# A mixture-of-experts layer on one core: rows come back by gathers that add into x, in place of gathers and additions on VectorE

## The reference

```python
x = x + 0.5 * ffn(layernorm(x), gate_w, experts)
x = x + attn(layernorm(x), W_in, conv_w, conv_b, A_log, D, W_out)
x = x + 0.5 * ffn(layernorm(x), gate_w, experts)

def ffn(x, gate_w, experts):               # B, N, D = 8, 2048, 256; E = 8; M = N // E = 256
    gates = sinkhorn(x @ gate_w)
    vals, idx = top_k(swapaxes(gates, -1, -2), M)      # each expert takes its 256 best tokens
    routed = x[b_idx, idx]
    outputs = (routed @ experts[e]) * vals
    return zeros_like(x).at[b_idx, idx].set(outputs)   # where several took one token, the last one stays
```

## Time and profile before

| | us |
|---|---|
| median of 3 runs | 3737.79 |
| the runs | 3739.79, 3737.79, 3731.17 |
| profiled execution, its own time | 3728.65 |
| its span, first to last instruction | 3727.1 |
| last layer (`ffn`) in it | from about 3315 to the end, 412 |
| busy in the span: PE, DVE, ACT, POOL | 2784.6, 3116.6, 2123.0, 1322.5 |

### The profile page before, as it was taken

How to read it: one execution, slowest core, us unless ns; L and a number is a source line. 1 busy time by engine, 2 the same in 40 slices (tenths; PEclk the granted TensorE clock), 3 DMA queues, 4 the chain that set the end, 5 groups by cost and what they waited for, 6 DMA issues and landing times. The chain is left out here.

```text
span 3727.1 us, 29733 instructions
## 1 busy us (share of the span) xinstructions
PE 2784.6 (75%) x9244; PEld 1530.2 (41%) x9244; DVE 3116.6 (84%) x2640; ACT 2123.0 (57%) x2277; POOL 1322.5 (35%) x897
## 2 busy tenths in 40 slices
PE   8703688899889799889988978987896687025653
PEld 4502333354345346435434534633442445024442
DVE  6797579999999999999999999999999566982222
ACT  6301467876877877787687787777767263001111
POOL 0002254436345344443734534450111100025665
PEclk9655799999999999999999989999998896557776
DMA  7202277688678778868867878886776462034666
GB/s 275 105 0 85 72 179 178 145 181 183 150 163 168 174 173 167 183 145 182 185 150 162 167 170 173 169 178 121 141 144 123 86 257 108 0 109 130 224 219 243
DMA packets 146619, 574.71 MB, mean 154 GB/s; under 512 B 22144, under 2 KB 73920, under 8 KB 99776
## 3 DMA queue, kind: packets, MB, share of 16 engines
q0 software_dynamic: 77136, 399.56, 51.6%
q1 hardware_dynamic: 69360, 173.68, 12.7%
HBM read 154.72 MB, written 117.51 MB: 73 GB/s over the span
## 5 line engine op out<-in xcount | busy, mean ns | idle before, releaser
L1143 DVE TENSOR_TENSOR_SCAN state<-state,drive 128x2048 f32<-128x2048 f32 x512 | 2224.3, 4404 | 54.0 <-ACT state L1341 53.7
L1341 ACT ACTIVATE state<-delta,neg_a 128x2048 f32<-128x2048 f32 x512 | 1019.4, 2005 | 230.3 <-DMA state<-state 95.7
L1555 PE MATMUL ps_states<-state,ident 128*128 128x512 f32 x1800 | 856.4, 621 | 109.5 <-DMA state<-state 94.8
L1034 POOL DMA_DIRECT2D state<-state x256 | 234.9, 919 | 1314.1 <-DVE state L1143 1303.7
L1491 PE MATMUL ps_proj<-x1t,w_in 128*128 128x512 f32 x1024 | 505.0, 637 | 90.6 <-ACT xc L1290 32.3
L1555 PEld LDWEIGHTS ps_states<-state,ident 128*128 128x128 f32 x1800 | 348.7, 200 | 516.5 <-issue 385.5
L1507 PE MATMUL ps_proj<-conv_in,tap 128*128 128x512 f32 x1024 | 488.1, 628 | 53.9 <-ACT conv_in L1262 33.0
L982 POOL DMA_INDIRECT picked<-normed_rows,slot_now x112 | 355.9, 3178 | 99.1 <-PE ps_rows L1472 55.0
L998 POOL DMA_INDIRECT x<-routed_rows,row_now x112 | 345.3, 3083 | 34.6 <-issue 34.6
L1491 PEld LDWEIGHTS ps_proj<-x1t,w_in 128*128 128x128 f32 x1024 | 202.8, 203 | 369.6 <-issue 265.8
L1507 PEld LDWEIGHTS ps_proj<-conv_in,tap 128*128 128x128 f32 x1024 | 203.8, 202 | 319.2 <-issue 280.3
(11 more groups left out here) (288 smaller groups left out, 3233.9 us busy)
## 6 DMA issues: line engine op xcount, KB each, us to landing
state<-state POOLq DMA_DIRECT2D x256, 1024.0 KB, 7.1
delta<-xc POOLq DMA_DIRECT2D x24, 1024.0 KB
normed_rows<-rows_in SPq DMA_DIRECT2D x8, 2048.0 KB
x_rows<-x SPq DMA_DIRECT2D x16, 1024.0 KB, 7.4
x_rows<-rows_out POOLq DMA_DIRECT2D x64, 256.0 KB, 8.3
normed_rows<-rows_mid SPq DMA_DIRECT2D x8, 2048.0 KB
f_total<-x_rows SPq DMA_DIRECT2D x8, 2048.0 KB
routed_rows<-f_routed SPq DMA_DIRECT2D x128, 128.0 KB
```

Source lines behind the costliest of these rows:

```text
L1034: nc.gpsimd.dma_start(out=state[held(q)][:], in_=state[held(q - 1)][:], accum_op=ALU.add).then_inc(pair_landed(b, q // 2)[0], 16)
L1143: nc.vector.tensor_tensor_scan(state[held(q)][:], state[held(q)][:], drive[j % 2][:], 0.0, ALU.mult, ALU.add).then_inc(state_ready, 1)
L1341: nc.scalar.activation(state[held(q)][:], delta[j % 2][:], ACT.Exp, scale=g.neg_a[:, j, n:n + 1]).then_inc(decay_ready, 1)
L1555: mm = nc.tensor.matmul(ps_sum[c][:], g.ident[:], state[held(q)][:, c * CH:(c + 1) * CH], start=(opening and n == 1), stop=(n == N - 1))
```

## The change

All of it is in `ffn`.

- The gather back writes no buffer: it has `compute_op=ALU.add` and its destination is the tile of x itself. `f_back`, its semaphores and DVE's additions are gone; a semaphore `joined` for each tile of x counts the gathers that have landed, and the store to the output waits for 16 of them.
- Picks and products have 16 buffers each (NX = NY = SL). `f_total` has four tiles (NTOT).
- After `BRING` = 22 slots, five picks go with four gathers back (`rows_due`); what is left, 44 gathers, follows the last pick. A gather back waits for nothing but, at the first of a batch, its tile of x and the stores of its slots.
- Index buffers are gone; the indirect transfers read `slot_token` and `token_row`.
- SP loads x for batch 0 at the start, for batches 1 to 3 twelve slots before the batch ahead has had its last gather, and for batches 4 to 7 five slots after the last gather of the batch whose tile they take. It stores a batch one slot after its last gather, batches 5 to 7 after all slots.

```diff
-    NX = NY = NK = 8
+    NX = NY = SL
     NT4 = 4
-    BRING, JOIN, LOAD = SL + 6, SL + 10, 3
+    NTOT = 4
+    BRING, STEP = SL + 6, 5
+    def rows_due(n):
+        return T * NB if n >= NB * SL else max(0, (n - BRING) * (STEP - 1) // STEP)
+    def slot_of(m):
+        return next(n for n in range(NB * SL + 1) if rows_due(n) >= (m + 1) * T)
...
+        def load_x(m):
+            if m >= NTOT:
+                sp.wait_ge(out_stored[m % NTOT], m // NTOT * 16)
+            sp.dma_start(total[m % NTOT][:], x_v[m]).then_inc(x_in[m % NTOT], 16)
+        def store_out(m):
+            sp.wait_ge(joined[m % NTOT], (m // NTOT + 1) * 16 * T)
+            sp.dma_start(out_v[m], total[m % NTOT][:]).then_inc(out_stored[m % NTOT], 16)
+        stores = {min(slot_of(m) + 1, NB * SL): m for m in range(NB) if slot_of(m) < NB * SL}
+        loads = {slot_of(m - 1) - 12 if m < NTOT else slot_of(m - NTOT) + 5: m for m in range(1, NB)}
...
+        def pick(b, s):
+            pool.wait_ge(turned, count(b * SL + s - NX + 1))
...
+                in_offset=bass.IndirectOffsetOnAxis(ap=g.slot_token[:, b, s:s + 1].bitcast(U32), axis=0)
+            ).then_inc(picked_in[s % NX], 16)
+        def bring(m, t):
+            if m == 0 and t == 0:
+                pool.wait_ge(table.ranked, 1)
+            if t == 0:
+                pool.wait_ge(x_in[m % NTOT], (m // NTOT + 1) * 16)
+                for k in range(NY):
+                    pool.wait_ge(routed_out[k], (m + 1) * 16 * (SL // NY))
...
+                out=total[m % NTOT][:, t, :], out_offset=None, in_=g.routed[m],
+                in_offset=bass.IndirectOffsetOnAxis(ap=g.token_row[:, m, t:t + 1].bitcast(U32), axis=0),
+                compute_op=ALU.add).then_inc(joined[m % NTOT], 16)
+        for n in range(NB * SL):
+            pick(n // SL, n % SL)
+            for v in range(rows_due(n), rows_due(n + 1)):
+                bring(v // T, v % T)
...
-                    dve.wait_ge(back_in[t % NK], (m * (T // NK) + t // NK + 1) * 16)
-                    nc.vector.tensor_tensor(total[m % 2][:, t, :], total[m % 2][:, t, :], back[t % NK][:], ALU.add
-                                            ).then_inc(added, 1)
```

More of the change, by code:

```diff
@@ L1701, in _ @@
         load_x(0)
[L1702 to L1705, removed]
+        for n in range(NB * SL):
+            b, s = n // SL, n % SL
+            sp.wait_ge(scaled, n + 1)
+            sp.dma_start(routed_v[b][s // NH, 1 + s % NH * P:1 + (s % NH + 1) * P, :],
+                         routed[s % NY][:]).then_inc(routed_out[s % NY], 16)
+            if n in stores:
+                store_out(stores[n])
+            if n in loads:
+                load_x(loads[n])
@@ L1707, in _ @@
+        for n in sorted(v for v in loads if v >= NB * SL):
+            load_x(loads[n])
+        for m in range(NB):
+            if m not in stores.values():
+                store_out(m)
+        for i in range(NTOT):
+            sp.wait_ge(out_stored[i], NB // NTOT * 16)
     @block.gpsimd
     def _(pool):
[L1709 to L1725, removed]
-                    pool.wait_ge(added, count(m * T + t - NK + 1))
-                    pool.sem_inc(g.passed_pool, 1)
-                    nc.gpsimd.indirect_dma_start(
-                        out=back[t % NK][:], out_offset=None, in_=g.routed[m],
-                        in_offset=bass.IndirectOffsetOnAxis(ap=row_now[m % 2][:, t:t + 1].bitcast(U32), axis=0)
-                    ).then_inc(back_in[t % NK], 16)
@@ L1749, in turn, with slots @@
-        def turn(b):
-            for s in range(SL):
-                if there(b):
-                    dve.wait_ge(turned, b * SL + s + 1)
-                    dve.wait_ge(product, count(b * SL + s - NT4 + 1))
-                    nc.vector.tensor_copy(picked_t[s % NT4][:].rearrange("p k n -> p (k n)"),
-                                          ps_turn[s % (NT4 if b else 2)][:, 0:KD * P]).then_inc(copied, 1)
+        def slots(b):
+            for s in range(SL):
+                dve.wait_ge(turned, b * SL + s + 1)
+                dve.wait_ge(product, count(b * SL + s - NT4 + 1))
+                nc.vector.tensor_copy(picked_t[s % NT4][:].rearrange("p k n -> p (k n)"),
+                                      ps_turn[s % (NT4 if b else 2)][:, 0:KD * P]).then_inc(copied, 1)
@@ L1761, in turn @@
                     dve.wait_ge(table.ranked, 1)
[L1762 to L1774 removed]
         split_tokens(nc, g, dve, table)
[L1776 removed]
+        for b in range(NB):
+            slots(b)
     @block.scalar
```

67 lines of the change are left out of this document (13 added, 54 removed).

## The result

The changed kernel took **3756.59 us** (median of 5 runs, 3749.73 to 3762.91), the kernel before 3731.17 on the same chip (3728.28 to 3739.79): a ratio of **1.0061 [1.0041, 1.0080]**, slower by 0.6%. Forecast were 3680 us, and the range ended at 3714. (The 3737.79 us that the forecast started from was the median of the first three of these five runs of the kernel before.) The profiled execution took 3757.09 us with a span of 3755.5, 28.4 us more than before.

The account below looks back on a forecast made before the run. POOL's issuing bounds the last layer: 3366.1 + 231 x 1.253 + 10.1 gives span 3665.6; 7.3 us of stops kept makes 3673, 54 us less. Between 3674.5 and 3683.5, forecast 3680 us; range 3663 to 3692, to 3714 with rivals 1 and 3.

Parts of the forecast that it names:

- POOL bounds the layer, 1.253 us a step: Last layer: POOL's issuing of 256 gathers at 1.253 us each needs 321 of the layer's 412 us.
- On POOL: 0.95 us for a plain gather, at least 0.85 for a direct transfer that accumulates; I take 0.95, between 0.85 and 1.14: POOL's price of an adding gather back: taken as 0.95 us; spans over 1.1 us would show the forecast wrong.
- The 45.8 us of waits for the addition go: Gathers back waiting for an f_back buffer until DVE's addition: without f_back no gather waits, saving 45.8 us.
- the forecast's 54 us: Whole span: 61.5 us less, with 7.3 us of stops kept, gives span 3673, 54 us less.
- Half of the other stops, 7.3 us, stay: POOL's 14.6 us of other stops: half kept for firsts of a batch and a full DMA.
- The start, "I leave 3366.1 as it is": First gather back still waits for tokens' ranks and batch 0's last stores, so it stays at 3366.1.
- DMA: DMA engines after 3366: 0.9 us per adding gather, sum 276 us under POOL's 299, full to 92%.
- Rival 1: DMA engines become the bound if an adding gather holds them over 1.08 us; time about 3700 or 3712; chance 0.16.
- Order, tables, four tiles, clock, end: Order worth part of 14.6 us, tables and tiles nothing, granted clock not below 0.72, end 10.1 us.
- Rival 2: Slower: adding gathers cost by rows on DMA, time 3782, or POOL takes 0.5 us longer per adding gather; chance 0.09.
- Rival 4: Stops only change names, gathers waiting for turn instead of addition, as picks land late; 3728 to 3740; chance 0.04.
- Rival 3: PE stays at the low clock level, 2.8 us per slot; span 3689, time 3696; chance 0.06.

Follow-up runs that it names:

- e12: Kernel before with six one-column memsets on POOL ahead of each gather; 3691.42 us, ratio to before 1.0063.
- e18: Changed kernel with plain gathers into 16 buffers, DVE additions, eight pick buffers, ten memsets before each gather back; 3689.32 us, 1.0057 to before.
- e15: Changed kernel without the addition in its gathers, with 17 one-column memsets on POOL ahead of each gather back; 3737.16 us, 1.0019 to before.
- e1: Changed kernel with the addition left out of the gathers back, all else kept; 3777.17 us, 1.0149 to before.
- e9: Kernel before, unchanged, run again on chip 14; 3668.53 us, ratio 1.0000.
- e4: Changed kernel with eight buffers for picks instead of 16; 3741.79 us, 1.0060 to before.
- e10: Changed kernel, unchanged, run again on chip 14; 3739.06 us, 1.0195 to before.
- e3: Changed kernel with the old order of one pick to one gather back; 3758.18 us, 1.0099 to before.
- e11: Changed kernel without the addition in its gathers back, run again on chip 14; 3660.85 us, 0.9983 to before.
- e13: Changed kernel with each adding gather bringing 64 rows instead of 128; 3735.50 us, 1.0017 to before.
- e14: Changed kernel with gathers back of 64 rows and without the addition; 3780.53 us, 1.0138 to before.
- e8: Changed kernel with eight pick buffers, each adding gather replaced by an adding direct transfer of 128 rows in table order; 3641.27 us, 0.9927 to before.
- e7: Changed kernel with plain gathers into 16 buffers, DVE additions, eight pick buffers, two memsets before every gather; 3663.04 us, 0.9988 to before.
- e2: Changed kernel with plain gathers into 16 f_back buffers and DVE's additions three slots later; 3738.51 us, 1.0040 to before.

## Why the prediction was wrong

- **POOL bounds the layer, 1.253 us a step**: right on chips of the second kind (e12, e18: a slower step lengthens the time by as much). On the first kind the step is the same, but late signals stop POOL on top of it.
- **The step that failed: "On POOL: 0.95 us for a plain gather, at least 0.85 for a direct transfer that accumulates; I take 0.95, between 0.85 and 1.14".** Measured: 1.548 us, beyond the 1.1 us that I had named as a sign of being wrong. Both ends were rows of operations that have one of the two properties each, indirect or adding; both together cost more than either. And of the earlier trace rows I took only the shortest, 0.85: its median is 0.97 and its longest 1.70. With 78.8 us more the sum would have read 3673 + 79 = 3752 us of span, and 3755.5 came. That it is so near is partly luck: the start was 10.7 us later than taken, and the 7.3 us of stops that I kept didn't come.
- **The 45.8 us of waits for the addition go**: they went, but the reason was wrong. I read "DVE comes late because it stands behind the copy of a slot picked only a few gathers before" from the earlier trace rows; the pick had landed and PE had turned it, but PE's signal came up to 9.4 us late. What removed the stops on the result's chip was, by e15, the slower pace of the adding gathers, that is, the very cost I had missed. So this step fails too, and would have made the forecast wrong by itself: with the addition's price taken out and all buffers kept, the stops grow on the first kind of chip (e1), and the forecast's 54 us weren't there to be had by buffers; on the second kind (e9) they weren't there at all.
- **Half of the other stops, 7.3 us, stay**: none stayed.
- **The start, "I leave 3366.1 as it is"**: 3376.78. Sixteen buffers let POOL issue picks for longer without a pause, and the hand-overs of the first slots came late; e4 (eight buffers) and e10 (a chip of the second kind) don't have it.
- **DMA**: 0.9 us per adding gather forecast, 0.91 measured. The share was 0.77 from the first gather back to the end and not 0.92: 0.77 x 379 us are 292 us of work where the sum had 276, spread over a longer path. Rival 1 needed over 1.08 us. The straight line worked out from the Trainium skill, "DMA: Bandwidth & Descriptors", section "Bandwidth", gave an estimated 1.3; the measurement decides against it here too. (This page of the Trainium skill calls transfers under 64 KB descriptor-dominated; these have 128 KB.)
- **Order, tables, four tiles, clock, end**: the order is worth nothing that e3 can tell; tables and tiles weren't tried one by one. PE's granted clock was 0.72 to 0.77, the end 10.5 us for 10.1, the last pick came at 3664.35 for 3602, since two steps took 3.13 us, not 2.51, and the start was late.
- **The rivals.** Rival 2 had the sign, and in its last sentences the place: "POOL taking 0.5 us longer per adding gather (61.5/128)". It took 0.6. I priced it into a rival of 0.09 because the direct transfer's 0.85 spoke against it; as an unpriced operation on the bounding engine it deserved an end of the range of its own. Rival 4 ("the stops only change their names") is near to what e1 shows, but its cause, late landings of picks, is wrong, the largest stops there are waits for stores and not for turns, and e1's 3777 us lie above its 3728 to 3740. Rival 3's low clock didn't come.

## What to carry to other kernels

When one engine's issuing is the bound, a change that moves work into its instructions has to be priced by that very instruction: a gather that adds cost POOL 1.55 us where a plain gather took 0.95 and a direct transfer that adds 1.02, and 128 of them outweighed all the waits they replaced. A wait names the instruction that came last, not why that came late: compare the end of the producer with the start of the consumer, and with the moment at which the semaphore was counted up, before calling something a shortage of buffers. And where the kernel before runs at two different times on different chips, a gain read from one profile may be that chip's own.

## What the runs showed of the hardware

- An indirect gather of 128 rows of 1 KB takes POOL 0.95 us, with the addition 1.55 (e10, e11); of 64 rows 0.90 and 1.42 (e13, e14). A direct transfer of 128 rows that adds takes 1.02 between picks (e8).
- The gap of 0.30 us between two of POOL's gathers holds two one-column memsets (0.14 us) at no cost (e7).
- On the chips of three of the six sets PE's signals reached DVE up to 25.0 us (e2) after its turn had ended by the profile, while POOL issued transfers 1.2 to 1.25 us apart. With steps of 1.28 and 1.85 us (changed kernel), or 1.25 and 1.67 us (e15) in turn, there was hardly any of it: late 0 to 11 us against 138 to 225. On chips 4, 8 and 14 no copy of any kernel began more than 0.04 us late. PE behind DVE's copies and SP behind ACT were never over 0.2 us late, on any chip.
